# Attention with 96 operand rows loaded at once, and its context normalised through memory and GpSimd instead of TensorE and VectorE

## The reference, cut to what matters

```python
h = _layernorm(x) * (1 + ca) + sa
q, k, v = heads(h @ Wq + bq), heads(h @ Wk + bk), heads(h @ Wv + bv)
scores = einsum('bhqd,bhkd->bhqk', q, k)
scores = (scores + rel_q + rel_k) / sqrt(D)     # rel_*: products with dist_emb[l - r + M - 1]
probs = softmax(scores, axis=-1)
ctx = einsum('bhqk,bhkd->bhqd', probs, v)       # back to B, S, E
x = x + ga * layernorm(ctx @ Wo + bo + h)
h = _layernorm(x) * (1 + cb) + sb
x = x + gb * sum_of_the_two_chosen_experts(h)
```

## Time and profile before

| reading | value |
|---|---|
| device time, median of 3 runs | 2888.73 us (2884.10 to 2892.21) |
| the profiled execution: its own time | 2886.97 us |
| its span from the first to the last instruction | 2885.2 us |
| busy over the span: PE, DVE, ACT, POOL | 2521.4, 2055.5, 1627.6, 1883.5 us (87%, 71%, 56%, 65%) |
| moved by DMA | 773.59 MB, 268 GB/s over the span |
| attention, stretch 1239 to 2239 us: PE, DVE, ACT, POOL | 966.09, 741.39, 800.47, 877.62 of 1000.00 us |
| experts, stretch 2306 to 2885 us: PE, DVE, ACT, POOL | 551.52, 453.05, 129.40, 335.08 of 579.00 us |

### The profile page before, as it was taken

The page is one execution under the profiler, slowest core; times in us unless marked ns, Lnnn a source line. Parts: engine busy times, 40 slices in busy tenths (PEclk is TensorE's granted clock), DMA queues, the critical chain, the costliest instruction groups (busy, mean ns, idle before and its releaser), DMA issues. The chain is left out here.

```text
span 2885.2 us, 53492 instructions
## 1 busy us (share of the span) xinstructions
PE 2521.4 (87%) x19084; PEld 1753.8 (61%) x19084; DVE 2055.5 (71%) x5771; ACT 1627.6 (56%) x2069; POOL 1883.5 (65%) x1535
## 2 busy tenths in 40 slices
PE   3988688788878888599999999999999499999998
PEld 1655477677767777366666666666666355555553
DVE  4767277667767777577777777777777388888885
ACT  1645556566556666277878778788877222222222
POOL 2333356565765564488888888888888356666664
PEclk7999777778778778599999999999999799999999
DMA  3688799999999999999999999999998312222210
GB/s 117 226 296 269 259 401 386 378 400 385 398 393 387 376 404 388 316 328 317 302 313 308 312 310 306 304 306 301 314 301 266 132 68 77 77 77 77 77 48 24
DMA packets 301960, 773.59 MB, mean 268 GB/s; under 512 B 37608, under 2 KB 104496, under 8 KB 258048
## 3 DMA queue, kind: packets, MB, share of 16 engines
q1 hardware_dynamic: 277152, 660.82, 66.6%
q10 hardware_dynamic: 17888, 86.27, 9.2%
q0 software_dynamic: 6656, 23.07, 2.3%
HBM read 417.39 MB, written 352.63 MB: 267 GB/s over the span
## 5 line engine op out<-in xcount | busy, mean ns | idle before, releaser
L952 POOL TENSOR_SCALAR t_neg<-t_neg,t_low 128x512 f32<-128x512 f32 x512 | 793.6, 1563 | 121.5 <-DVE t_low L1153 117.2
L1153 DVE CUSTOM_DVE_ANT_1 t_neg<-t_ps,t_r 128x512 f32<-128x512 f32 x1024 | 667.6, 686 | 250.5 <-issue 245.5
L1215 ACT ACTIVATE t_eT<-t_pt 128x1024 f32<-128x1024 f32 x512 | 524.3, 1024 | 211.6 <-PE t_pt L1072 211.0
L1072 PE MATMUL t_pt<-t_ident,t_neg 128*128 128x128 f32 x4096 | 617.3, 273 | 4.7 <-POOL t_neg L952 4.2
L1072 PEld LDWEIGHTS t_pt<-t_ident,t_neg 128*128 128x128 f32 x4096 | 516.4, 142 | 82.9 <-POOL t_neg L952 5.9
L1537 PE MATMUL e_pX<-e_we,e_h2T 128*128 128x512 f32 x1024 | 455.8, 596 | 14.3 <-DVE e_even L1745 14.3
L1060 PE MATMUL t_ps<-t_kb,t_qa 96*128 96x512 bf16 x1024 | 399.1, 390 | 62.0 <-DVE t_low L1153 37.2
L831 DVE TENSOR_TENSOR d_r<-d_pq,d_r 128x1024 f32<-128x1024 f32 x256 | 299.6, 1219 | 139.0 <-ACT d_r L804 103.8
L1205 ACT ACTIVATE t_neg<-t_neg,t_low 128x512 f32<-128x512 f32 x512 | 369.2, 721 | 46.3 <-DVE t_low L1153 46.3
L831 DVE TENSOR_TENSOR ad_nat<-d_pq,ad_nat 128x1024 f32<-128x1024 f32 x256 | 298.6, 1218 | 121.0 <-ACT ad_nat L804 99.5
L706 POOL COPY ad_nat<-ad_nat 32x2048 f32<-32x2048 f32 (+1 forms) x156 | 294.3, 1886 | 104.6 <-DMA ad_nat<-q_by_place_scratch 98.3
(11 more groups left out here) (156 smaller groups left out, 3269.6 us busy)
## 6 DMA issues: line engine op xcount, KB each, us to landing
t_r<-r_scratch SPq DMA_DIRECT2D x1024, 256.0 KB, 6.5
r_scratch<-d_r SPq DMA_DIRECT2D x128, 1024.0 KB, 9.3
r_scratch<-ad_nat SPq DMA_DIRECT2D x128, 1024.0 KB, 7.0
ad_nat<-q_by_place_scratch ACTq DMA_DIRECT2D x78, 256.0 KB, 6.3
q_rows_scratch<-a_part SPq DMA_DIRECT2D x16, 768.0 KB, 4.7
k_rows_scratch<-a_part SPq DMA_DIRECT2D x16, 768.0 KB, 6.7
q_by_place_scratch<-ad_nat SPq DMA_DIRECT2D x6, 2048.0 KB, 16.8
k_by_place_scratch<-ad_nat SPq DMA_DIRECT2D x6, 2048.0 KB, 19.4
```

The source lines that it names most:

```text
L952: nc.gpsimd.tensor_scalar(neg[:, j % RING, t, :], neg[:, j % RING, t, :], low[:, j % RING, t:t + 1], None, ALU.subtract).then_inc(pool_sub, 1)
L1072: last = nc.tensor.transpose(p_t[t // 2][:, t % 2, c, :], neg[:, j % RING, t, c * P:(c + 1) * P], ident[:])
L1153: nc.vector.tensor_tensor_reduce(out=neg[:, j % RING, t, :].rearrange("p (c r) -> p c r", r=TB), in0=p_s[t % 2][:].rearrange("p (c r) -> p ...
L1215: nc.scalar.activation(to, p_t[half][:], ACT.Exp, scale=(1.0 if half else -1.0)).then_inc(exped, 1)
```

## The change

**Row loads.** `load_rows` brings all 96 rows of both operands: 24 DMAs per batch, each of 16 rows for 8 heads (16x4096, 131 KB), and writes each part into every sixth partition, so that row d of part p lies in partition 6d + p. Those of the first batch are on ScalarE's queue. All later ones are on SP's, two behind the `t_r` loads of each head, from head 6 of a batch to head 1 of the next. Both copies are gone, and TensorE waits for the loads themselves (`batch_loaded`).

**Context.** SP stores `t_cs` as `empty` left it, three groups later, together with a store of 4 rows of sums (4x512). `sums`, `widen` (on both engines) and `scale` are gone, and `p_i` with them. Once a batch SP loads the batch's sums as 128x64, VectorE's `invert` takes the reciprocal of them all, and SP stores it to `inv_d`.

**Experts.** SP's `load(b)` also brings the inverses, each row of 512 to 16 partitions (16 DMAs). GpSimd's `scale(b)` multiplies `e_cT` by them (128x1024), at the start of a batch for the batch after next, and `project` waits for that. The last batch's sums are inverted in this stage.

```diff
+        def load_rows(engine, b, half, pair, x):
+
+            tensor, parts = ((qa, A_PARTS), (kb, B_PARTS))[x]
+            first = H // 2 * half
+            at = b % 2 * H + first
+            engine.dma_start(tensor[pair:ROWS:NPAIR, 0, at:at + H // 2, :].rearrange("d h w -> d (h w)"),
+                             rows_d[x][b, parts[pair] * D:(parts[pair] + 1) * D, first:first + H // 2
+                                       ].rearrange("d h w -> d (h w)")).then_inc(batch_loaded[b % 2][half], 16)
...
-                def widen(G):
-
-                    pool.wait_ge(inverted, G + 1)
-                    later(pool, spread, G)
-                    nc.gpsimd.tensor_copy(wide[:], inv[:].rearrange("p t j -> p (t j)").unsqueeze(2)
-                                          .to_broadcast([P, GT, CT])).then_inc(widened, 1)
...
                 def store(b, k):
 
-                    sp.wait_ge(scaled, BG * b + k + 1)
                     G = BG * b + k
+                    sp.wait_ge(emptied, G + 1)
                     for j in range(GH):
                         row = (GH * k + j) * D
                         sp.dma_start(cT_d[b, row:row + D, :], cs[j * CT:j * CT + D, G % CS, :]
                                      ).then_inc(ctx_stored[G % CS], 16)
 
+                    sp.dma_start(sums_d[b, GH * k:GH * (k + 1), :], cs[D:P:CT, G % CS, :]).then_inc(ctx_stored[G % CS], 16)
+
+                def load_sums(b):
+
+                    for i in range(CS):
+                        sp.wait_ge(ctx_stored[i], STORE * ((BG * b + BG - 1 - i) // CS + 1))
+                    later(sp, inverted, b)
+                    sp.dma_start(sums[:], sums_d[b].rearrange("h s -> (h s)").rearrange("(p x) -> p x", p=P)
+                                 ).then_inc(sums_loaded, 16)
...
-                        if k % GT == 4 and (not fixed or 0 <= G < NGR):
-                            sums(G)
-                        if k % GT == 9 and (not fixed or 0 <= G < NGR):
-                            widen(G)
...
-                            if j % GH == GH - 1 and not (last and s == H // U - 1 and j == U - 1):
-                                pe.wait_ge(q_copied, 2 * (BG * b + (U * s + j) // GH + 2))
-                                pe.wait_ge(k_copied, BG * b + (U * s + j) // GH + 2)
+                            if j == U - 1 and not (last and s == H // U - 1):
+
+                                pe.wait_ge(batch_loaded[(b + s) % 2][1 - s], HALF * ((b + s) // 2 + 1))
...
+                def invert(b):
+
+                    dve.wait_ge(sums_loaded, 16 * (b + 1))
+                    later(dve, inv_stored, 16 * b)
+                    nc.vector.reciprocal(inv[:], sums[:]).then_inc(inverted, 1)
...
-                        if t == 1 and n % 2 == 0 and b < nb:
-                            copy_q(b, m)
-                        G = 2 * step + k // GT - 2
-                        if k % GT == 5 and (not fixed or 0 <= G < NGR):
-                            invert(G)
-                        if k % GT == 11 and (not fixed or 0 <= G < NGR):
-                            scale(G)
...
+                        if t == 3 and n % H == H - 2 and H <= n < NH:
+                            invert(n // H - 1)
...
                     sp.dma_start(cT[:, u], cT_d[b].rearrange("(k p) l -> p k l", p=P)).then_inc(ctx_loaded[u], 16)
+                    if b == nb - 1:
+                        sp.wait_ge(inv_stored, 16)
+                    for row in range(H):
+                        k, part = divmod(row, P // D)
+                        sp.dma_start(ib[part * D:(part + 1) * D, u, k, :], inv_d[b, row].partition_broadcast(D)
+                                     ).then_inc(ctx_loaded[u], 16)
...
+                def scale(b):
+                    u = b % 2
+
+                    pool.wait_ge(ctx_loaded[u], 16 * (H + 1) * (b // 2 + 1))
+                    nc.gpsimd.tensor_tensor(cT[:, u], cT[:, u], ib[:, u], ALU.mult).then_inc(ctx_scaled, 1)
...
                 for b in range(nb):
+                    if b + 2 < nb:
+                        scale(b + 2)
                     for t in range(TT - 1):
                         finish(b, t)
...
-                    pe.wait_ge(ctx_loaded[u], 16 * (b // 2 + 1))
+                    pe.wait_ge(ctx_scaled, b + 1)
```

More of the change, by code:

```diff
@@ L1250, in batch @@
                             head(H // U * b + s, j)
[L1251 to L1256 removed]
                 for half in range(2):
[L1259 to L1260 removed]
+                    for pair in range(NPAIR):
+                        for x in range(2):
+                            load_rows(act, 0, half, pair, x)
                 batch(0)
```

146 lines of the change are left out of this document (55 added, 91 removed).

## The result

The changed kernel took **3050.78 us** (median of 4 runs, 3041.62 to 3066.17) against 2888.48 (4 runs, 2884.10 to 2892.21): ratio 1.0568, 95% interval 1.0517 to 1.0618. It is 162 us slower where 43 us less was forecast, and outside the forecast's range. The profiled executions span 3055.2 and 2885.2 us, and the 170 us between them have four parts. VectorE's 1024 sums of attention start at 1202.3 before and at 1206.8 after (4.5 us more). They run from 1202.3 to 2245.3 before and from 1206.8 to 2343.3 after (93.5 us more). From the last sum to TensorE's first projection of the experts stage it is 25.6 and 28.5 us (2.9 more). From there to the end it is 614.3 and 683.4 us (69.1 more).

The account below looks back on a forecast made before the run. The prediction took TensorE's own queue in attention as the bound. Its terms, -46.7 - 3 + 0 + 6.5 + 2 = -41.2 us, from 2886.97 us gave 2845.8 us, range 2825 to 2866.

Parts of the forecast that it names:

- Attention, TensorE (-46.7): Attention: each group loses 1.93 us of transposes and waits and gets back 1.2, so 46.7 us less in 64 groups.
- The new waits: Attention: TensorE would newly wait per group 0.4 us for GpSimd, 0.5 for ScalarE and perhaps 0.15 for VectorE, together 1.05.
- Attention, the transfers (0): Attention: the 24 row loads and other new issues on SP's queue would fit within 62.3 us a batch, costing nothing.
- Start (+-4) and end (-3) of attention: Attention's ends: later bytes against missing copies, 0 between -4 and +4; last scaling and transposes gone, two more issues, -3 us.
- The experts' start (+6.5): Start of the experts stage: 16 issues of inverse rows ahead of e_mod's load cost 6.5 us, between 3 and 10.
- The scaling (+2): Experts stage: GpSimd's scaling fits its 4.9 us gap; pieces of VectorE's normalisation caught cost 2 us, between 0 and 20.
- SP's queue becomes the bound: Rival, attention: held-up issues make t_r late; at 0.60 us an issue a batch takes 68.4 us, total 2943; chance 0.10.
- The scaling collides: Rival, experts stage: the scaling collides with VectorE, 3 us in each of 14 batches, total 2886 us; chance 0.03.
- the waits of VectorE for `t_r`: Sign in attention: no wait of VectorE for t_r was expected; such waits would show the prediction wrong.
- a longer experts' period: Sign in the experts stage: the same period as before was expected; a growing one would show the prediction wrong.

Follow-up runs that it names:

- e8: The changed kernel without the row loads of batches 2 to 15, so later batches reuse rows of batch 0 or 1: 2918.9 us.
- e16: The changed kernel with only the k rows loaded from batch 2 on, 12 loads a batch on SP's queue instead of 24: 2920.8 us.
- e5: The changed kernel with each 16-row part loaded into 16 neighbouring partitions instead of every sixth: 3223.4 us.
- e2: The changed kernel with the row loads on ScalarE's queue, two behind each of a batch's first 12 heads, instead of SP's: 2939.1 us.
- e4: The kernel before with only the new row loads on SP's queue and no copies, keeping the old normalisation and experts stage: 2984.8 us.
- e7: The kernel before with two more 64-byte loads per head on SP's queue in attention, 116 issues a batch instead of 84: 2888.8 us.
- e1: The changed kernel with GpSimd's scaling cut into four instructions of 128x256: 3038.6 us.
- e10: The changed kernel with 24 useless identity transposes per experts batch, to fill TensorE's idle gap: 3016.9 us.

## Why the prediction was wrong

The sum of the forecast was -41.2 us, and the profiled executions differ by +170. Its terms one by one:

*Attention, TensorE (-46.7): right, but it never came to count.* e8 and e16 have a batch of 62.07 us, 15.52 a group, where the forecast had 15.57. The new waits are there as well. In e8, 1320 to 2200 us or 56.7 groups, TensorE waits 0.61 us a group for GpSimd (forecast 0.4), 0.31 for ScalarE (0.5) and 0.07 for VectorE (0.15), 1.0 together against 1.05:

```profile
PEld t_pt L1076 <- POOL t_neg L954: 34.8, 99, 0.4
PE t_pt L1076 <- ACT t_eT L1174: 17.7, 57, 0.3
PEld t_ps L1064 <- DVE t_low L1135: 4.1, 14, 0.3
```

*Attention, the transfers (0): the step that failed, +9.8 us a batch against 62.07.* The text let 24 row loads stand in SP's queue among the position terms at no cost, for two reasons, and neither held. The first was the price. "I take the first, since its rows lie all over the array" took a load at 0.33 us, by a stretch's 393 GB/s, and the other 17.9 MB of a batch at the same rate, 45.4 us. On the scale of the DMA share a load is 0.62 to 0.70 us (e8 and e16) and the rest 52.1: the peak of a 4 us stretch was taken for a rate that lasts. Nor was 0.63 the most that a load could cost, since e5, with neighbours, lies 20.2 us a batch above 62.07, 0.84 us for each of its 24. The second was the queue: "a short backlog hides and a lasting one doesn't". It lasted: VectorE idled 207 us ahead of first tiles, and position terms took up to 17.8 us to land (14.1 before). This was the larger part: 1.9 us a batch stay with the loads in ScalarE's queue (e2), 7.9 come with SP's, which moves 296 GB/s where the two move 331. By what the one queue loses isn't shown.

*Start (+-4) and end (-3) of attention:* +4.5, just outside, and -2.9 (from the last sum to the experts stage's first load, 18.4 us before and 15.5 after).

*The experts' start (+6.5):* the 16 issues take 7.4 us (2360.21 to 2367.62), `e_mod` lands after 6.19 instead of 9.23, and GpSimd's first sum comes 16.3 instead of 11.7 us behind the stage's first issue: +4.6, inside 3 to 10.

```profile
2358.78 0.40 SPq L1352
...
2360.21 0.46 SPq L1343
...
2367.20 0.42 SPq L1343
...
2368.84 6.19 DMA e_mod<-mod_scratch
```

*The scaling (+2): the second step that failed.* The scaling did fit into GpSimd's gap (2617.18 to 2619.54). But the gap was read on GpSimd, and on VectorE only the big pieces of the normalisation were held against it. VectorE was in its small steps there, each waited for by the next, and one of them was stopped for as long as GpSimd's instruction ran (2.3 us). The big pieces cost 0.8 us more, by being pushed beside `finish`. The term came out at 5.1 us in each of the 13 periods from the third batch on, and some 2 of it were TensorE's clock, which stood in no term. The Trainium skill, page "SBUF — State Buffer", section "SBUF: two separate sides", says that VectorE (in its faster two-port modes, or with two operands in SBUF while GpSimd reads SBUF) and GpSimd share one pair of ports, that whoever starts first has it for the whole instruction and that the other is blocked. The durations agree, 2.48 us beside 2.36, and 0.60 to 0.66 beside pieces of 0.7. Who had it first isn't shown: the record of the stopped VectorE instruction even begins 0.09 us ahead of GpSimd's.

*The rivals.* "SP's queue becomes the bound" (0.10) had the sign, the place and nearly the price: it wrote down 0.60 us an issue, and 71.84 us for 114 are 0.63. Its reasons hold in part. The position terms did come late, but not because more bytes go per microsecond (296 GB/s, against 308 before in the same stretch), and the number of issues doesn't decide: e4 took as long with 104, and 116 with short ones among them left e7 at 65.2. "The scaling collides" (0.03) had 3 us a batch, which is VectorE's share of the 5.1, and no clock. Both came at once. Of the signs named ahead, the waits of VectorE for `t_r` and a longer experts' period both appeared, and both had been called proof of an error.

## What to carry to other kernels

A transfer's price has to be taken from the mean over a stage at its real mix, not from its best 4 us, and the whole stage's transfers set against the span that the engines want. With room left, loads were free (12 of them cost nothing). With the DMA engines' share at 1.03 it mattered most in which queue they stood: 24 cost 1.9 us a batch in a queue of their own and 9.8 in that of the urgent loads. The busy share of DMA engines doesn't show this; the bytes per second do. A GpSimd instruction put into a gap of GpSimd's has to be held against what VectorE does in the same microseconds, the tiniest steps above all; the place for such work was a gap of VectorE's own. And a delay that leaves TensorE idle can cost again behind it, at the lower clock: here 3.96 us of idle time were followed by 2.7 us more for the next 16 matmuls.

## What the runs showed of the hardware

- A load of 16 rows of 8 KB into every sixth partition took 0.62 to 0.70 us of the DMA engines' time (e8 against e16); with 16 neighbours a batch with 24 of them took 10.5 us longer (82.3 against 71.8).
- One queue for everything moved 296 GB/s at a DMA share of 1.04, the same traffic from two queues 331 at 1.03 (e2). A share above 1 went with 258 GB/s in e5: it doesn't tell what is moved.
- A VectorE instruction on 128x4 elements took 2.48 us beside a GpSimd instruction of 2.36 us, and 0.17 alone; beside four instructions of some 0.7 us three such steps took 0.60 to 0.66 each (e1).
- TensorE's clock stood at 1.00 behind 0.97 and 1.37 us of idle time, and fell to 0.50 behind 3.96; shortening the gap with useless transposes took the experts' period from 41.0 to 39.2 us (e10).
